# Experts by groups: rows sent to the slots of their two chosen expert groups

## The reference

```
scores = sigmoid(x @ router_w.T)                     # 16 experts, in 4 groups of 4
s      = scores + bias
group_score = sum of the two largest s in a group    # the 2 best groups of 4 stay
topk_idx = the 4 largest s among those 2 groups' 8 experts
tw       = scores[topk_idx] / sum * 2.5              # combine: 0 for the 12 experts not taken
y_e      = (silu(x @ gate_w[e]) * (x @ up_w[e])) @ down_w[e]
out      = x_before + sum_e combine[t,e] * y_e + shared(x)     # shared: two more experts, for all tokens
```

## Time and profile before

| | us |
|---|---|
| median of 3 runs | 2140.08 |
| lowest, highest | 2134.15, 2143.28 |
| the profiled execution | 2129.31 |
| its span | 2127.5 |
| first and second attention run with choice | 0 to about 1287 |
| relu steps | about 1287 to 1426 |
| expert steps | 1426 to 2127.5 |

### The profile page before, as it was taken

The page is one execution under the profiler, slowest core; times in us unless marked ns, Lnnn a source line. Parts: engine busy times, 40 slices in busy tenths (PEclk is TensorE's granted clock), DMA queues, the critical chain, the costliest instruction groups (busy, mean ns, idle before and its releaser), DMA issues. The chain is left out here.

```text
span 2127.5 us, 52756 instructions
## 1 busy us (share of the span) xinstructions
PE 1974.6 (93%) x19220; PEld 1530.4 (72%) x19220; DVE 1629.4 (77%) x4569; ACT 1063.6 (50%) x2180; POOL 465.4 (22%) x520
## 2 busy tenths in 40 slices
PE   7999995888869999999999998989999999999998
PEld 4666673677736666666666665767888888888887
DVE  5777775777538888888888884678888878888886
ACT  5656652666625555555455443544444444444442
POOL 1111111111002232323223223762111211111111
PEclk9999997999969999999999998999999999999999
DMA  3000000000000000001000002000000000000000
GB/s 128 31 30 20 30 10 1 1 1 1 1 20 2 0 0 0 0 1 32 20 30 30 20 10 68 1 1 6 6 6 5 10 6 5 6 6 10 6 5 11
DMA packets 27409, 30.50 MB, mean 14 GB/s; under 512 B 1952, under 2 KB 20640, under 8 KB 27040
## 3 DMA queue, kind: packets, MB, share of 16 engines
q1 hardware_dynamic: 27296, 29.18, 4.2%
HBM read 24.98 MB, written 4.19 MB: 14 GB/s over the span
## 5 line engine op out<-in xcount | busy, mean ns | idle before, releaser
L491 DVE TENSOR_REDUCE mx<-ps 128x8 f32<-128x512 f32 x384 | 261.9, 682 | 162.7 <-PE ps L681 162.5
L398 ACT ACTIVATE ex<-ps 128x512 f32<-128x512 f32 x384 | 230.2, 600 | 259.1 <-PE ps L699 257.0
L1125 ACT ACTIVATE y_res<-ps 128x512 f32<-128x512 f32 x288 | 172.4, 599 | 355.4 <-PE ps L1211 355.3
L1193 PEld LDWEIGHTS ps<-down,y_res 128*128 128x128 f32 x2048 | 267.2, 191 | 25.0 <-issue 3.0
L699 PE MATMUL ps<-pack,sh 128*128 128x128 f32 x1536 | 249.5, 284 | 29.7 <-DVE sh L493 28.8
L493 DVE TENSOR_TENSOR sh<-ps,mx 128x512 f32<-128x512 f32 x384 | 265.4, 691 | 13.2
L1193 PE MATMUL ps<-down,y_res 128*128 128x128 f32 x2048 | 270.7, 275 | 1.4 <-DVE y_res L1479 1.4
L1461 DVE TENSOR_TENSOR y_res<-ps,y_res 128x512 f32<-128x512 f32 x288 | 197.6, 686 | 80.4 <-PE ps L1211 66.0
L715 PEld LDWEIGHTS ps<-vblk,ex 128*64 128x64 f32 x6144 | 211.5, 138 | 65.0 <-issue 65.0
L699 PEld LDWEIGHTS ps<-pack,sh 128*128 128x128 f32 x1536 | 168.1, 141 | 121.2 <-issue 62.2
L715 PE MATMUL ps<-vblk,ex 128*64 128x32 f32 x6144 | 254.4, 226 | 0.0
(11 more groups left out here) (237 smaller groups left out, 3388.6 us busy)
## 6 DMA issues: line engine op xcount, KB each, us to landing
ctxT<-in_ctx SPq DMA_DIRECT2D x32, 256.0 KB, 2.8
x_res<-in_x SPq DMA_DIRECT2D x16, 256.0 KB, 2.8
kmi<-in_key_mask SPq DMA_DIRECT2D x16, 256.0 KB, 3.3
out<-y_res SPq DMA_DIRECT2D x16, 256.0 KB, 2.3
pack<-in_pack SPq DMA_DIRECT2D x1, 2053.0 KB, 10.2
wqkv<-in_wqkv SPq DMA_DIRECT2D x1, 1536.0 KB, 10.8
gate<-in_gate SPq DMA_DIRECT2D x6, 192.0 KB, 3.6
up<-in_up SPq DMA_DIRECT2D x6, 192.0 KB, 3.8
```

Of the source, the lines that this page charges most:

```text
L398: nc.scalar.activation(ex[:, u % 2], UB[u % 4].rearrange("p (c n) -> p c n", n=P), ACT.Exp).then_inc(e_ready, 1)
L491: nc.vector.tensor_reduce(mx[:, u % 2], sc, AX.X, ALU.max).then_inc(max_done, 1)
L1193: last = nc.tensor.matmul(YB[k % 2][:, t * D:(t + 1) * D], act_[:, k % 3, t * P:(t + 1) * P], down[:, k, :], start=True, stop=True)
```

## The change

**Only the two chosen groups' experts are computed.** During the relu steps each group of tokens is also normed into `xw` (128 features and the 16 weights, RW = 144 columns a row), turned, multiplied by the router (`logits`) and, in batches of 5, 5 and 6 groups, routed (`route`, now with 20 or 24 times 16 elements a row). Tokens are taken in two chunks, groups 0 to 4 and 5 to 15. `count` and `find_slots` give each token two slots, one in a tile of each of its chosen expert groups; a tile is 512 slots that all belong to one expert group, 13 tiles for the first chunk and 25 for the second (38 in all, whether full or not). GpSimd `send`s the rows of a chunk to their slots in DRAM by indirect DMAs, one per 128 rows and choice: 40 and 88.

**The tile loop** (38 tiles) loads a tile's rows and its group's gate, up and down weights, splits both, runs four jobs, weighs and adds them into `acc` and stores the tile to DRAM. GpSimd `fetch`es the two results of each row back by indirect DMAs, 8 per group of tokens, the first five groups from tile 15 on, the other eleven (88 DMAs) behind the loop. **The shared experts** come last, two jobs for each of the 16 groups, with the sum and the output. The shape of a job stays what it was; 38 x 4 + 16 x 2 = 184 jobs stand where 16 x 18 = 288 stood. The weighing of the first expert of a tile is ScalarE's, of the other three VectorE's.

**Attention.** The first group's k, q and v get banks of their own, so that q, k and v don't wait for each other's copies, and in the second run `vblk` is cleared behind the first norm's statistics.

```diff
+CHUNKS = ((0, 5), (5, NG))
+BATCHES = ((0, 5), (5, 10), (10, NG))
+ROUTE0, COUNT_AT, SLOTS0, SEND_AT, SENDS = (8, 9, 10, 11), 11, 11, 12, 3
+ROUTE1, COUNT1_AT, SLOTS1, SEND1_AT, FETCH_AT = (0, 1, 2, 3), 2, 4, 5, 15
 # SyncE
+            def load_weights(tile):
+                if tile in FROM:
+                    sp.wait_ge(placing, (chunk_of(tile) + 1) * NS)
+                if tile >= 2:
+                    sp.wait_ge(w_split, tile)
+                    sp.wait_ge(y_ready, results(tile - 1))
+                e = sp.value_load(tid_i[0:1, tile:tile + 1], min_val=0, max_val=EG - 1)
+                here = bass.ds(e * GE + SH, GE)
+                sp.dma_start(raw[:, tile % 2, 0], gate_in[:, here, :]).then_inc(w_loaded[tile % 2], 16)
+                sp.dma_start(raw[:, tile % 2, 1], up_in[:, here, :]).then_inc(w_loaded[tile % 2], 16)
+                sp.dma_start(down[:, tile % 2], down_in[:, here, :]).then_inc(w_loaded[tile % 2], 16)
...
+            load(0)
+            load(1)
+            for tile in range(NTT):
+                sp.wait_ge(weighed, results(tile + 1))
+                sp.dma_start(slots_of(done, tile), acc[:, tile % 2]).then_inc(stored[tile % 2], 16)
+                if tile + 2 < NTT:
+                    load(tile + 2)                   # load_weights, then load_rows
 # GpSimd
+            for g in range(NG):
+                relu_step(g)
+                if g >= SEND_AT:
+                    send(0, SENDS * (g - SEND_AT), SENDS)
+            norm_power(NG - 1)
+            send(0, SENDS * (NG - SEND_AT), 4 * NG)
+            split_weights(0)
+            for tile in range(NTT):
+                if tile + 1 < NTT:
+                    split_weights(tile + 1)
+                if SEND1_AT <= tile < FROM[1] - 1:
+                    n = -(-(CHUNKS[1][1] - CHUNKS[1][0]) * TILES // (FROM[1] - 1 - SEND1_AT))
+                    send(1, n * (tile - SEND1_AT), n)
...
+            for g in range(*CHUNKS[1]):
+                fetch(g)
 # TensorE
+            for tile in range(NTT):
+                for e in range(GE):
+                    k = tile * GE + e
+                    products(tile, k, e)
+                    if k >= 2:
+                        expert_rows(k - 2)
+                    if e == 1 and tile + 1 != FROM[1]:
+                        turn_rows(tile + 1)          # waits for the rows of tile + 1
 # VectorE
+            for tile in range(NTT):
+                for e in range(GE):
+                    k = tile * GE + e
+                    if k >= 3:
+                        weigh(k - 3)
+                    product(k, k - 2)
+                    if e == 2 and tile + 1 != FROM[1]:
+                        low_rows(tile + 1)
+                    if e == 3 and tile + 1 < NTT and tile + 1 != FROM[1]:
+                        own_weights(tile + 1)
+                    for i, at in enumerate(ROUTE1):
+                        if e == 1 and tile == at:
+                            route(2, (2 * i, 2 * i + 1))
 # attention, TensorE, first group
-                if n > 0:
+                bank = FIRST_BANK[what] if start else PREP
+                if start:
+                    if n > L.nr("xT"):
+                        pe.wait_ge(prep_copied, L.nr("xT") + 1)
+                elif n > 0:
                     pe.wait_ge(prep_copied, nth(g, NP, n - 1))
```

More of the change, by code:

```diff
@@ L877, in late_phase @@
[L877 to L890, removed]
@@ L1238, in r_prep, with count @@
-            def r_prep(g, s):
-                pe.wait_ge(yn_ready, nth(g))
-                for t in range(TILES):
-                    last = nc.tensor.transpose(RXB[s][:, t * P:(t + 1) * P], yn[:, s, t, :], C["ident"])
-                last.then_inc(yT_ready, 1)
-            def r_step(g, s, first, more):
+            def count(c, seen):
+                lo, hi = CHUNKS[c]
+                pe.wait_ge(routing, NR * (sum(b[1] <= hi for b in BATCHES) - 1) + 17)
+                pe.wait_ge(exp_done, seen)
+                n = EG * (hi - lo) * TILES
+                chosen = gin[:, lo * TILES:hi * TILES, :].rearrange("p t g -> p (t g)")
+                nc.tensor.matmul(RANK[:, 0:n], C["tri"], chosen, start=True, stop=True)
+                nc.tensor.matmul(TOTAL[:, 0:n], C["ones"], chosen, start=True, stop=True).then_inc(counted, 1)
@@ new lines, in expert_rows @@
+            def expert_rows(k):
+                tile, e = k // GE, k % GE
+                pe.wait_ge(act_ready, k + 1)
+                if k < 2:
+                    pe.wait_ge(summed, NG)
+                else:
+                    pe.wait_ge(weighed, k - 1)
+                for t in range(TILES):
+                    last = nc.tensor.matmul(YB[k % 2][:, t * D:(t + 1) * D], act_[k % 3][:, t * P:(t + 1) * P],
+                                            down[:, tile % 2, e], start=True, stop=True)
+                last.then_inc(y_ready, 1)
@@ new lines, in shared_rows @@
+            def shared_rows(g):
+                k = jobs(NTT + g)
+                pe.wait_ge(act_ready, k + SH)
+                if g < 2:
+                    pe.wait_ge(weighed, GE * NTT)
+                else:
+                    pe.wait_ge(row_summed, g - 1)
+                for t in range(TILES):
+                    for j in range(SH):
+                        last = nc.tensor.matmul(YB[g % 2][:, t * D:(t + 1) * D], act_[(k + j) % 3][:, t * P:(t + 1) * P],
+                                                shared[:, 2, j], start=(j == 0), stop=(j == SH - 1))
+                last.then_inc(y_ready, 1)
@@ L1278, in _ @@
+            expert_rows(NTT * GE - 2)
+            expert_rows(NTT * GE - 1)
+            for g in range(NG):
+                for j in range(SH):
+                    products(NTT + g, jobs(NTT + g) + j, j)
+                    if j == 0 and g + 1 < NG:
+                        turn_rows(NTT + g + 1)
+                    if j == 0 and g >= 1:
+                        shared_rows(g - 1)
+            shared_rows(NG - 1)
         @block.vector
         def _(dve):
-            def add_to_x(g, s):
+            V = nc.vector
@@ new lines, in _ @@
+            for k in range(GE * NTT - 3, GE * NTT):
+                weigh(k)
+            for g in range(NG):
+                for j in range(SH):
+                    k = jobs(NTT + g) + j
+                    old = k - 3
+                    need = old + 1 if old < GE * NTT else results(NTT + (old - GE * NTT) // SH + 1)
+                    product(k, need)
+                    if j == 0 and g + 1 < NG:
+                        low_rows(NTT + g + 1)
+                if g >= 1:
+                    shared_sum(g - 1)
```

1153 lines of the change are left out of this document (683 added, 470 removed).

## The result

The changed kernel takes 2425.06 us (median of 4 runs, 2419.12 to 2427.13), the kernel before 2137.11 (median of 4) beside it: ratio 1.135, interval 1.132 to 1.139, slower. The forecast was 2390 in a range of 2270 to 2580. The profiled run has a span of 2421.1 us, where the prediction's sum made it 2380.

What follows compares the result with a forecast made beforehand. TensorE bounds the kernel before. On its span of 2127.5: attention -8, relu +16 +17 +22, transition +44, experts +162 give 2380; 11 to the median and 1.8 around the span give 2390 us, range 2270 to 2580.

Steps and rivals of the forecast that it cites:

- the wait: Tile loop: TensorE waits for rows loaded behind the previous stores, 7.9 us a tile (6.4 to 10.7), 36 times, 284 us.
- the clock's share: Tile loop: products behind each wait start at half clock, 2.2 us a tile (0 to 5), 79 us in all.
- Relu steps and transition: Relu steps: TensorE work +16, routing +17, sends in steps 12 to 15 +22; last relu product to first tile +44.
- The tile loop: 38 tiles: work 364, wait 284, clock 79, third routing batch and second slot search 19; sum 746 us.
- The tail: After the loop: 88 fetches at 1.2 us, 106, plus last weighing, store, landing, adds and output: 117 us.
- the split weights hide behind two jobs: Tile loop: splitting the weights (ScalarE 1.2, GpSimd 2 x 1.28 us) has two jobs' time, 4.6 us, so is hidden.
- Sends in tiles 5 to 11: GpSimd's 14 sends at 1.2 us plus 2.6, 19.4 us, fit a tile of 19.7: no cost at this price.
- rival 2: GpSimd's indirect DMAs bound the kernel: 2760 us at 2.8 us each, 2580 at 2.0; chance 20%.
- the short wait: Tile loop: the wait's low end, 6.4 us with no register load time and landing 2.8; -54 us.
- Rival 1: Tile loop: the round trip is hidden, 363 us of wait and clock fall away, 2030 us; chance 5%.
- Rival 3: Tile loop: the clock holds (-79) or the wait is at its short end (-54), 2310 to 2335 us; chance 15%.
- Rival 4: Tile loop: the clock stays at 1.2 GHz throughout, +265, 2655 us; chance 5%.

Runs made afterwards that it cites:

- the filler: Changed kernel plus 34 products nobody reads on TensorE in tiles 5 to 36 (not 12), where it waits for rows: 2365.95 us, ratio 1.108.
- the new tail: Changed kernel with VectorE adding fetched groups 5 and 6 behind shared steps 3 and 5: 2518.06 us, ratio 1.181.
- the early kernels: Changed kernel with rows, gate and up loaded before the store's wait: 2115.08 us, on chip 1 2166.93; with additions moved too, 2157.38 and 2164.91.
- 80 in a row: Early loads and moved additions, plus six groups in the first chunk and splits on VectorE in tiles that send: 2200.81 us, ratio 1.030.
- the four kernels on chip 3: Changed kernel with rows, gate and up early (2115.08 us), rows alone early (2328.73), gate and up alone early (2324.14), or useless TensorE products added (2365.95).
- the kernel without indirect DMAs on chip 9: Kernel before with the attention edits alone: 2126.18 us, ratio 0.9959.

## Why the prediction was right, and where it was off

The verdict, the range and the mechanism held: the tile period was forecast at 19.7 us and is 20.4, the wait 7.9 and is 8.2 in the median, the clock's share 2.2 and is 2.5, with 36 such waits. The likeliest value was 35 us low (41 of the span). By terms:
- Attention -8: measured -9. Relu steps and transition: the first expert product was forecast at 1517 (1426 - 8 + 16 + 17 + 22 + 44) and came at 1511.45. The sum is right and its places are not, and that is luck in part. TensorE's last relu products ended at 1446.5 and not at 1473, and from there to the first expert product it was 65 us and not 44. GpSimd's steps with sends follow each other at 14 to 15.5 us (forecast 14.3), but TensorE didn't wait for it: it went on at 8.8 a step and stood still behind the last. VectorE's routing stretched no step from 8 to 11 either. It came due in one wait: the router product of step 12 waits 18.8 us (+17 was forecast for the routing) until VectorE, busy 20.3 of the 22.9 us up to there, has read the counts out of the bank that the product writes. What an earlier reading would bring wasn't tried.
- **The tile loop was mis-sized by 28 us** (774 for 746), nearly all of it 36 x 0.7 in wait and clock. In the tile shown, SyncE's part of the round trip was right (1.17 from the store to the gate's issue, 1.41 to the rows'; 2.58 for my 2.6), TensorE's end to the store was 1.2 for 1.6, and the landing with TensorE's start 4.8 for 3.7. I had taken a value between 2.8 and 4.4 since the burst is paced by its issues. The landing alone has a median of 4.3 over all 38 tiles, so the upper end was the right one. With the weights early the median is 3.2, so the loads ahead of the rows make the difference.
- **The tail was mis-sized by 18** (135.6 for 117): 88 x 1.25 = 110 instead of 106, and a pause of 12.1 that I didn't look for. The third group fetched needs the buffer of the first, whose addition stands behind five shared steps in VectorE's order.
- That the split weights hide behind two jobs held: TensorE waits nowhere in the tile loop for a split of weights. It says nothing of the weights' load, which runs beside the rows' chain and is as long. Whoever moved only the rows on the strength of it would gain 96 us and not 310.
- Sends in tiles 5 to 11 "nothing at this price" was right by 0.3 us of slack, and only where there are no stalls.
- Two slips in the working change nothing: 24 sends at 0.8 us more are +19 and not +25, so rival 2 at 2.0 us and the upper end of the range are 2574, and the short wait adds up to 6.3 and not 6.4.

Rival 1 fell (the wait decides, and 310 us go with it). Rival 3 fell with the filler: the clock doesn't hold. Rival 4 fell by the product at 0.39 from 1702. Rival 2 in its own form fell, 1.26 us an issue. But its sign, tiles 5 to 11 above 25 us, came in the changed kernel on chip 1 and in the one with the new tail on chip 9, by a mechanism that I hadn't named: there ScalarE and VectorE stand still while GpSimd sends. Its 2580 was nearer to the 2532 of chip 1 than my 2390. That 2532 lies in my range too is luck, since the sum has no term for it.

So the cause is shown: the loads behind the store cost 310 us, more than the 288 by which the change is slower (the kernel before took 2137.1 beside both runs), and 365 between two kernels of one set on chip 1, where the change is 399 us slower. Without them the change brings 22 us (1%) on one chip and loses 34 on another.

## What to carry to other kernels

A load that needs a buffer freed two tiles ago shouldn't stand in an in-order queue behind a store of the present tile: look for the oldest event that each DMA needs, and issue it there. When two chains of like length end in one place, removing one shows a third of the gain; try both before judging. Don't let GpSimd issue a long run of indirect DMAs beside work of ScalarE and VectorE; keep something that paces it, and time the kernel on more than one chip.

## What the runs showed of the hardware

- An indirect DMA of 128 rows holds GpSimd 0.96 us with 0.30 between two: 1.26 us, sending or (1.25) fetching. From issue to landing it takes 2.3 us (median of the changed kernel's 128 sends), so the next is issued while one is under way. The Trainium skill (DMA: Bandwidth & Descriptors, anatomy of one DMA, SWDGE) has some 2 us fixed, mostly completion. The trace agrees with the size, and by these rows the completion isn't the issuing engine's time.
- Idle TensorE is not free of cost: 34 useless products of 512 columns took 8.0 us and gave 59 us back.
- While GpSimd issues indirect DMAs one after another, ScalarE and VectorE start instructions late on two of the chips. They stand idle up to 7 us (12.5 in the early kernels) a time with 14 sends a tile, up to 17 in the tail, and 49.5 with 80 in a row. The traces of the kernel before, of the changed kernel's first run and of the four kernels on chip 3 have no such wait at all, nor has the kernel without indirect DMAs on chip 9. In the early kernel on chip 1 the waits stand where GpSimd sends or fetches (1607 to 1722, 1778 to 1851, from 2026 on), and none between 1512 and 1595 or between 1871 and 2006, where it does neither. That it isn't the program is shown by the changed kernel (2425 and 2532) and by the early loads (2115 and 2167). What holds the engines stays open: TensorE goes on within a microsecond once VectorE has run, and the kernel before, with no indirect DMA, takes 2133 to 2137 beside all of them.
